# A two-layer transformer kernel: TensorE's order of work written out in layer 1's attention, and the projection's first step taken in parts

## The chip, the cores and the metric

The kernel runs on one core of one Trainium2 chip. The metric is the time of one execution on the device in microseconds (us). TensorE, VectorE, ScalarE and GpSimd (PE, DVE, ACT and POOL in the rows) compute, each from its own list of instructions; SyncE (SP) issues the transfers used here. They meet only at semaphores.

## The reference

Two layers over 1024 tokens of width 512. Each adds an attention and a feed-forward network, both computed from the same normalised input, to the residual:

```python
x = L0_attn_hidden_states
xn = _layernorm(x, axis=-1)
x = x + _L0_attn_ref(xn, ...) + _L0_ffn_ref(xn, ...)
xn = _layernorm(x, axis=-1)
x = x + _L1_attn_ref(xn, ...) + _L1_ffn_ref(xn, ...)
```

The change stands in layer 1, whose attention has 32 heads of 16 numbers; four heads share a key and a value:

```python
scores = jnp.einsum('bhqd,bhkd->bhqk', q, k)
scores = jnp.where(causal[None, None], -jnp.inf, scores)
weights = jax.nn.softmax(scores * (1.0 / HD ** 0.5), axis=-1)
ctx = jnp.einsum('bhqk,bhkd->bhqd', weights, v)
return jnp.dot(ctx, Wo) + bo
```

## The kernel before

Products that need the accuracy of float32 are made of three products of halves: every operand is split into a high part (ScalarE casts it) and a low part (GpSimd or VectorE subtracts), and `mm3` (lines 155 to 157) issues high by high, low by high and high by low.

**From layer 0's output to layer 1's queries** (`outputs_to_queries`). 32 steps, 16 for each half of the tokens, multiply the attention's output with a folded weight. A step has four slots to choose from (`s = k % 4`). ScalarE casts the outputs `ch` (line 2063) and then the weight `oh_w` (line 2064); the second cast raises `split_done`. VectorE then forms `cl` (line 2137) and GpSimd `ol_w` (line 2021). TensorE waits for both and issues twelve matmuls, three for each of four blocks of 128 tokens. Nothing can be multiplied before the first step's parts stand.

**Layer 1's attention** (`grouped_attention`). Eight rounds, one for each group `g` of four heads. A round does two things at once:

- For a group ahead it finds the largest score of every query. `score(g, v)` (line 2412) is a matmul for unit `v`, one of 4 heads by 8 tiles of 128 queries; a tile sees 128 to 1024 keys. VectorE reduces it (`maximum`, line 2505). Tiles come in the order of widths 640, 512, 768, 384, 896, 256, 1024, 128, over and over. The four wide ones (640, 768, 896, 1024) share one PSUM slot, the narrow ones another, so a score waits until the maximum of the score but one before it has been taken (`max_done`). A score wider than 512 is two matmuls.
- For its own group it computes the weights and the result in 12 steps `s`. `keys(g, s, p)` (line 2435) computes scores again, turned, for two heads; ScalarE takes the exponential (line 2526) from the same two banks, and `keys` of the next step waits for it. GpSimd clears the masked corner in 8 of 12 steps (line 2566). `weigh(g, s)` (line 2451) multiplies with the values, two steps later (`LAG`), and adds the sums of the weights in spare columns. The steps are 512, 384, 256, 128 queries wide, then five of 512 and 384, 256, 128.

TensorE's order is made by a rule: in step `s` stand `SHARE[s]` scores, about a third after `keys(g, s, 0)`, a third after `keys(g, s, 1)`, and the rest after `weigh`. With `SHARE = [4, 3, 2, 1, 4, 3, 4, 3, 4, 2, 1, 1]` a round holds 32 scores, and scores run 4 units ahead of the round.

At step 9 `turn` (line 2421) transposes the 32 columns of maxima into bank 0, `take_shift` on ScalarE copies them (line 2533), and SyncE carries them by four transfers into the queries' extra row (`shift_group`, line 1870). The next round's first `keys` waits for these. SyncE's loop for each round is: spread the sums of the group before (second half), then of this group (first half), then the shift, then the inverted sums (`spread_scales`), then the loads of the group three ahead. VectorE inverts a group's sums with `invert_sums` (line 2274) after its 25th maximum (`v == 24`). After the last step of rounds 3, 5 and 7 GpSimd scales two finished groups (`scale_heads`, line 2281). The last round has no scores; it begins the feed-forward network instead, one `mm3` for each step.

## Time and profile before

| | us |
|---|---|
| median of 3 runs | 1690.13 |
| lowest and highest run | 1683.23, 1690.16 |
| the profiled execution, its own time | 1686.73 |
| its span, first to last instruction | 1685.0 |

| stretch of the span (us) | what runs |
|---|---|
| 1068 to 1156 | the 32 steps of the projection |
| 1217 to 1488 | the eight rounds of layer 1's attention |
| 1489 to 1685 | layer 1's feed-forward network |

Of the whole span TensorE is busy 96%, VectorE 64%, ScalarE 51% and GpSimd 42%. The granted TensorE clock is 0.985 of full speed on average. "Busy" counts an engine's running instructions; TensorE's matmuls overlap, and their ends are modelled, so the starts of consecutive matmuls tell more than their lengths.

### The profile page before, as it was taken

To read this page: it belongs to the slowest core of one execution; us is meant where nothing else is said; L and a number is where in the kernel's file an instruction comes from. 1 tells how busy PE (TensorE), PEld (TensorE's weight loads), DVE (VectorE), ACT (ScalarE), POOL (GpSimd) and SP (SyncE) were. 2 spreads that over 40 slices of the span, in tenths; PEclk is the share of its full clock that TensorE was granted. 3 is DMA by queue.
4 is the path that set the end of the run, shared out by engine and by line. 5 is a ranking of instruction groups with operands and counts; after the bars stand their busy time and mean duration, and the time that the engine had idled before them with its cause. 6 is when DMAs were issued, how large, how long until landed. Compare 5 with 4: busy or idle time off the path is not lost. (4 is left out here: it accounts for less than half of the span.)

```text
span 1685.0 us, 27527 instructions
## 1 busy us (share of the span) xinstructions
PE 1610.0 (96%) x8810; PEld 1221.0 (72%) x8810; DVE 1083.1 (64%) x2489; ACT 851.7 (51%) x1592; POOL 714.2 (42%) x741
## 2 busy tenths in 40 slices
PE   6899999999998999999999999899899999999998
PEld 5688887788776777777777777687655555568887
DVE  3656657999937878887788877355767767310222
ACT  3456556444325655666566656443155655643321
POOL 1212213444656665666676665575011122232321
PEclk9999999999998999999999999999989999999999
DMA  8522323221110000001000100672523323131111
GB/s 247 187 80 82 94 70 102 65 62 37 57 32 7 27 25 20 20 26 32 20 20 26 33 13 14 195 223 68 156 56 62 72 59 69 49 102 51 51 50 50
DMA packets 113023, 114.17 MB, mean 68 GB/s; under 512 B 39777, under 2 KB 72001, under 8 KB 112897
## 3 DMA queue, kind: packets, MB, share of 16 engines
q1 hardware_dynamic: 110592, 108.40, 23.0%
q10 hardware_dynamic: 2304, 4.20, 0.7%
q8 instruction: 67, 1.10, 0.3%
q14 instruction: 60, 0.48, 0.1%
HBM read 83.97 MB, written 28.44 MB: 67 GB/s over the span
## 5 line engine op out<-in xcount | busy, mean ns | idle before, releaser
L1579 ACT ACTIVATE a_p<-a_sm,a_nmax 128x640 f32<-128x640 f32 (+7 forms) x256 | 198.5, 776 | 109.5 <-PE ps L1398 58.7
L1656 POOL TENSOR_SCALAR a_p<-a_p,a_rinv 128x640 f32<-128x640 f32 (+7 forms) x256 | 189.8, 750 | 125.8 <-DVE a_rinv L1490 125.7
L1479 DVE CUSTOM_DVE_ANT_0 a_sm<-ps,maskb 128x640 f32<-128x640 f32 (+7 forms) x256 | 189.6, 750 | 41.7 <-PE ps L1383 39.8
L2505 DVE CUSTOM_DVE_ANT_0 ga_sm<-ps,strip 128x640 f32<-128x640 f32 (+1 forms) x224 | 163.1, 754 | 72.0 <-PE ps L2412 70.5
L2526 ACT ACTIVATE ga_pt<-ps 128x1024 f32<-128x1024 f32 (+1 forms) x192 | 147.9, 810 | 113.2 <-PE ps L2435 112.2
L1398 PE MATMUL ps<-ident,a_p 128*128 128x128 f32 x1152 | 163.0, 276 | 2.7 <-DVE a_pt L1502 1.8
L2566 POOL TENSOR_SCALAR_AFFINE_SELECT ga_pt<-ga_pt 128x512 f32<-128x512 f32 x64 | 40.6, 635 | 265.7 <-ACT ga_pt L2526 265.5
L1398 PEld LDWEIGHTS ps<-ident,a_p 128*128 128x128 f32 x1152 | 133.2, 141 | 19.3 <-issue 6.6
L952 DVE SCALAR_TENSOR_TENSOR idx<-ix_r,ix_sgc,idx 128x256 f32<-128x256 f32 (+6 forms) x105 | 90.7, 884 | 74.2 <-ACT ix_r L918 74.2
L1418 PE MATMUL ps<-a_pt,vst 128*64 128x512 f32 (+3 forms) x768 | 134.2, 492 | 1.9 <-DVE a_pt L1502 1.1
L918 ACT ACTIVATE ix_r<-ps,ix_awc 128x256 f32<-128x256 f32 (+6 forms) x112 | 89.2, 798 | 83.1 <-PE ps L851 69.8
L1502 DVE COPY a_pt<-ps 128x128 f32<-128x128 f32 (+3 forms) x256 | 120.5, 482 | 14.5 <-PE ps L1398 14.2
L1383 PE MATMUL ps<-kh,lq_qh 128*128 128x512 f32 (+4 forms) x384 | 123.2, 375 | 6.7 <-POOL lq_ql L1793 3.6
L2412 PE MATMUL ps<-ga_kst,ga_qst 96*128 96x320 f32 (+1 forms) x336 | 107.5, 387 | 18.2 <-DVE ga_nmax L2505 15.6
L2412 PEld LDWEIGHTS ps<-ga_kst,ga_qst 96*128 96x128 f32 x336 | 58.0, 196 | 89.2 <-DVE ga_nmax L2505 64.0
L1383 PE MATMUL ps<-kh,lq_ql 128*128 128x512 f32 (+4 forms) x384 | 112.4, 347 | 0.0
L1383 PE MATMUL ps<-kl,lq_qh 128*128 128x512 f32 (+4 forms) x384 | 112.3, 347 | 0.0
L1594 ACT COPY a_pt<-ps 128x512 f32<-128x512 f32 x128 | 74.2, 580 | 64.8 <-PE ps L1398 63.6
L1418 PEld LDWEIGHTS ps<-a_pt,vst 128*64 128x64 f32 x768 | 51.5, 136 | 73.3 <-issue 64.9
L2435 PE MATMUL ps<-ga_qst,ga_kst 98*128 98x512 f32 (+3 forms) x384 | 99.2, 356 | 1.3 <-DMA ga_qst<-idx 1.3
L1780 POOL TENSOR_TENSOR lq_t<-lq_t 128x512 f32<-128x512 f32 x63 | 81.2, 1289 | 41.7 <-DVE lq_t L1775 41.7
L1793 POOL TENSOR_TENSOR lq_ql<-lq_t,lq_qh 128x512 fp32r<-128x512 f32 x64 | 82.3, 1286 | 28.1 <-ACT lq_qh L1787 28.0
(315 smaller groups left out, 3953.4 us busy)
## 6 DMA issues: line engine op xcount, KB each, us to landing
idx<-ctx_d SPq DMA_DIRECT2D x32, 256.0 KB, 3.2
idx<-wvo_d SPq DMA_DIRECT2D x32, 256.0 KB, 3.8
ga_qst<-qkd SPq DMA_DIRECT2D x42, 128.0 KB, 4.5
f_wr<-in_L_ffn_w SPq DMA_DIRECT2D x18, 256.0 KB, 2.7
x<-in_L_attn_hidden_states SPq DMA_DIRECT2D x16, 256.0 KB, 4.1
op_wo<-in_L_attn_o_w SPq DMA_DIRECT2D x8, 512.0 KB, 5.3
ix_w<-in_L_attn_idx_wq_w SPq DMA_DIRECT2D x64, 64.0 KB, 1.9
ix_fo<-in_L_attn_o_w SPq DMA_DIRECT2D x8, 512.0 KB, 4.1
```

The source lines that it names most:

```text
L952: ins = dve.scalar_tensor_tensor(out=acc, in0=r[:, u % 2, 0:W], scalar=sgc[:, a, t:t + 1], in1=acc, op0=ALU.mult, op1=ALU.add)
L1383: ins = pe.matmul(slots[kind][:, at0:at0 + k1 - k0], l[:, a, at], r[:, k0:k1], start=j == 0, stop=j == 2, skip_group_check=True)
L1398: ins = pe.transpose(ps[:, bank_t[n % NT], k * P:(k + 1) * P], p[kind][:, v // 2 % 2, (j0 + k) * P:(j0 + k + 1) * P], qwork["ident"][:, :])
L1418: ins = pe.matmul(ps[64 * a:64 * a + 64, bank_c, off:HALF], vst[:, j, :], pt[half][:, (2 * i + a) % NBUF, j, off:HALF], start=j == 0, stop ...
L1479: dve.tensor_tensor_reduce(out=in_row(sm[kind][:, 0:w], w), in0=in_banks(slots[kind], w), in1=in_row(maskb[:, MASK_OFF[t]:MASK_OFF[t + 1]] ...
L1502: dve.tensor_copy(pt[g][:, buf, j0:j0 + m, at], bank4(ps, bank_t[n % NT])[:, 0:m]).then_inc(pt_done[n % NT], 1)
L1579: act.activation(p[kind][:, v // 2 % 2, 0:w], sm[kind][:, 0:w], ACT.Exp, bias=nmax[:, v % 4:v % 4 + 1], scale=-1.0, accum_out=rsum[:, v % ...
L1656: pool.tensor_scalar(mine, mine, rinv[:, v % 4:v % 4 + 1], 1.0, ALU.mult, ALU.mult).then_inc(norm_done, 1)
L2412: ins = pe.matmul(slots[kind][:, at0:at0 + k1 - k0], qst[0:KQ, b, h // 2, t * P:(t + 1) * P], kst[0:KQ, b, h % 2, k0:k1], start=True, stop ...
L2435: ins = pe.matmul(ps[:, 2 * p + a, 0:q1 - q0], kst[0:KQ + 2, b, a, j * P:(j + 1) * P], qst[0:KQ + 2, b, p, q0:q1], start=True, stop=True)
L2505: dve.tensor_tensor_reduce(out=in_row(sm[kind][:, 0:w], w), in0=in_banks(slots[kind], w), in1=in_row(strip[:, S - w:], w), scale=-1.0, sca ...
L2526: act.activation(pt[:, n % RING, 2 * p:2 * p + 2, off:HALF], ps[:, 2 * p:2 * p + 2, 0:q1 - q0], ACT.Exp, scale=SCALE).then_inc(exp_done[p], 1)
```

## The change

Layer 0's attention already has its order written out before the change; the diff doesn't touch it. In layer 1:

1. The rule with `SHARE` goes. The 12 steps of a round are written out line by line: where each `keys`, score, `weigh` and `turn` stands.
2. Scores run further ahead. Four (`LEAD`) are issued ahead of round 0, and four more are added at the ends of the steps in `CATCH_UP`, three in round 0 and one in round 1, so that from round 2 on they run 8 units ahead.
3. `turn` stands ahead of `keys(g, 9, 1)`, `take_shift` between the two exponentials of step 9.
4. `weigh(g, 1)` stands one step earlier, in step 2, and step 3 has none.
5. `invert_sums` follows the 31st maximum (`v == 30`), and GpSimd's `scale_heads` stands ahead of step 4 of rounds 3, 5 and 7 rather than after step 11.
6. In the projection ScalarE casts the weight first and signals it by a semaphore of its own (`wvh_done`), for which GpSimd waits; the first step's twelve matmuls are issued by parts, four as soon as the high parts stand, four after `cl`, four after `ol_w`.

```diff
@@ outputs_to_queries @@
-                    pool.wait_ge(split_done[s], START + u + 1)
+                    pool.wait_ge(wvh_done[s], START + u + 1)
                     pool.tensor_tensor(ol_w[:, s], wr[:, s], f32(oh_w[:, s]), ALU.subtract).then_inc(wvl_done[s], 1)
...
-                    act.copy(ch[:, s], cr[:, s])
-                    act.copy(oh_w[:, s], wr[:, s]).then_inc(split_done[s], 1)
+                    act.copy(oh_w[:, s], wr[:, s]).then_inc(wvh_done[s], 1)
+                    act.copy(ch[:, s], cr[:, s]).then_inc(split_done[s], 1)
...
-                for half, k, s, u in steps:
+                def first_step():
+
+                    pe.wait_ge(wvh_done[0], START + 1)
+                    pe.wait_ge(split_done[0], START + 1)
+                    for t in range(4):
+                        pe.matmul(ps[:, t, :], ch[:, 0, t * P:(t + 1) * P], oh_w[:, 0], start=True, stop=False,
+                                  skip_group_check=True)
+                    pe.wait_ge(cl_done[0], START + 1)
...
+                    pe.wait_ge(wvl_done[0], START + 1)
...
+                first_step()
+                for half, k, s, u in steps[1:]:
@@ grouped_attention @@
-    LEAD = 3
+    LEAD = 4
+    TURN_AT = 9
...
-    SHARE = [4, 3, 2, 1, 4, 3, 4, 3, 4, 2, 1, 1]
+    CATCH_UP = ((0, 1), (0, 4), (0, 7), (1, 4))
...
-                        pe.wait_ge(exp_done[0], START + (g - 1) * NSTEP + NSTEP - LEAD + 1)
+                        pe.wait_ge(exp_done[0], START + (g - 1) * NSTEP + TURN_AT + 1)
...
+                for g in range(G1):
+                    keys(g, 0, 0)
+                    keys(g, 0, 1)
+                    next_score()
+                    next_score()
+                    next_weigh()
+                    end_step(g, 0)
...
-                        if v == 24 and g >= 2:
+                        if v == 30 and g >= 2:
                             invert_sums(dve, g - 2, rest)
...
                         exponential(g, s, 0)
+                        if s == TURN_AT and g + 1 < G1:
+                            take_shift(g + 1)
                         exponential(g, s, 1)
-                        if s == NSTEP - LEAD and g + 1 < G1:
-                            take_shift(g + 1)
...
+                        if s == 4 and g >= 3 and g % 2 == 1:
+                            scale_heads(pool, g // 2 - 1, ctxn, rest)
...
-                    if g >= 3 and g % 2 == 1:
-                        scale_heads(pool, g // 2 - 1, ctxn, rest)
```

The round as written out, in short: K is a `keys` of one pair of heads, W a `weigh`, T the `turn`, and a number is the width of a score, as they fall in rounds 2 to 5. Before, the same rounds read as in the second column.

| step | after | before |
|---|---|---|
| 0 | K K 640 512 W | K 896 K 256 W 1024 128 |
| 1 | K 768 K 384 W | K 640 K 512 W 768 |
| 2 | K 896 K 256 W 1024 W | K 384 K W 896 |
| 3 | K 128 K 640 512 | K K W 256 |
| 4 | K K 768 W 384 | K 1024 K 128 W 640 512 |
| 5 | K 896 K 256 W | K 768 K 384 W 896 |
| 6 | K 1024 128 K W 640 512 | K 256 K 1024 W 128 640 |
| 7 | K K 768 W 384 | K 512 K 768 W 384 |
| 8 | K 896 K W 256 1024 | K 896 K 256 W 1024 128 |
| 9 | K 128 W 640 T 512 K | K 640 K T W 512 |
| 10 | K 768 W 384 896 K | K K W 768 |
| 11 | K 256 W 1024 K 128 | K K W 384 |

TensorE at the start of round 3, from the first `keys` to the end of step 1. `ps<-ga_qst,ga_kst` is a `keys`, `ps<-ga_kst,ga_qst` a score, `ps<-ga_pt,v` a `weigh`. First as it stands before, then as it stands now:

```order
L2435 MATMUL ps<-ga_qst,ga_kst 128x512 x2
L2412 MATMUL ps<-ga_kst,ga_qst 128x512
L2412 MATMUL ps<-ga_kst,ga_qst 128x384
L2435 MATMUL ps<-ga_qst,ga_kst 128x512 x2
L2412 MATMUL ps<-ga_kst,ga_qst 128x256
L2451 MATMUL ps<-ga_pt,v 32x256 x4
L2412 MATMUL ps<-ga_kst,ga_qst 128x512 x2
L2412 MATMUL ps<-ga_kst,ga_qst 128x128
L2435 MATMUL ps<-ga_qst,ga_kst 128x384 x2
L2412 MATMUL ps<-ga_kst,ga_qst 128x320 x2
L2435 MATMUL ps<-ga_qst,ga_kst 128x384 x2
L2412 MATMUL ps<-ga_kst,ga_qst 128x512
```

```order
L2456 MATMUL ps<-ga_qst,ga_kst 128x512 x4
L2432 MATMUL ps<-ga_kst,ga_qst 128x320 x2
L2432 MATMUL ps<-ga_kst,ga_qst 128x512
L2472 MATMUL ps<-ga_pt,v 32x256 x4
L2456 MATMUL ps<-ga_qst,ga_kst 128x384 x2
L2432 MATMUL ps<-ga_kst,ga_qst 128x512
L2432 MATMUL ps<-ga_kst,ga_qst 128x256
L2456 MATMUL ps<-ga_qst,ga_kst 128x384 x2
L2432 MATMUL ps<-ga_kst,ga_qst 128x384
L2472 MATMUL ps<-ga_pt,v 32x128 x4
```

Before, only a 128-wide score and one `keys` stand between the 1024-wide score (512 x2) and the next wide one (320 x2); now the round starts with both `keys`, and its first wide score is followed by the 512-wide one, a `weigh` and a `keys` before the next wide one.

TensorE around the `turn` (`ps<-ident,ga_nmax`) in step 9 of round 3, before and now:

```order
L2412 MATMUL ps<-ga_kst,ga_qst 128x512 x2
L2412 MATMUL ps<-ga_kst,ga_qst 128x128
L2435 MATMUL ps<-ga_qst,ga_kst 128x384 x2
L2412 MATMUL ps<-ga_kst,ga_qst 128x320 x2
L2435 MATMUL ps<-ga_qst,ga_kst 128x384 x2
L2421 MATMUL ps<-ident,ga_nmax 32x128
L2451 MATMUL ps<-ga_pt,v 32x512 x4
```

```order
L2432 MATMUL ps<-ga_kst,ga_qst 128x512 x2
L2456 MATMUL ps<-ga_qst,ga_kst 128x384 x2
L2432 MATMUL ps<-ga_kst,ga_qst 128x128
L2472 MATMUL ps<-ga_pt,v 32x512 x4
L2432 MATMUL ps<-ga_kst,ga_qst 128x320 x2
L2442 MATMUL ps<-ident,ga_nmax 32x128
L2432 MATMUL ps<-ga_kst,ga_qst 128x512
L2456 MATMUL ps<-ga_qst,ga_kst 128x384 x2
```

The `weigh` has moved between the 1024-wide score and the next wide one, and the `turn` has moved ahead of step 9's second `keys`.

## Rows read from the trace of the kernel before

**Rows 1.** Stretches: length; PE, PEld, DVE, ACT, POOL busy (instructions); clock; DMA share; GB/s.

```profile
1222.00:1255.00 33.00, 30.70 (x152) 17.87 (x151) 21.75 (x59) 17.62 (x23) 3.80 (x6) 0.83 0.22 43
...
1288.00:1321.00 33.00, 30.41 (x197) 17.26 (x193) 23.75 (x65) 19.23 (x26) 5.03 (x8) 1.00 0.37 71
```

**Rows 2.** TensorE in order of time, one round: start, length, engine, line, operation, idle before.

```profile
1292.87 0.63 PE L2435 MATMUL ps<-ga_qst,ga_kst 98*128 98x512 f32 x2
1293.33 0.28 PE L2412 MATMUL ps<-ga_kst,ga_qst 96*128 96x256 f32 x1
1293.55 0.64 PE L2451 MATMUL ps<-ga_pt,v 128*32 128x256 f32 x8
1294.22 0.79 PE L2412 MATMUL ps<-ga_kst,ga_qst 96*128 96x512 f32 x3
1294.84 0.57 PE L2435 MATMUL ps<-ga_qst,ga_kst 98*128 98x384 f32 x2
1296.27 0.56 PE L2412 MATMUL ps<-ga_kst,ga_qst 96*128 96x320 f32 x2 [0.86 <-DVE ga_nmax L2505]
...
1304.41 0.79 PE L2412 MATMUL ps<-ga_kst,ga_qst 96*128 96x320 f32 x3 [0.23 <-DVE ga_nmax L2505]
...
1305.89 0.62 PE L2412 MATMUL ps<-ga_kst,ga_qst 96*128 96x512 f32 x2 [0.24 <-DVE ga_nmax L2505]
...
1307.57 0.68 PE L2412 MATMUL ps<-ga_kst,ga_qst 96*128 96x512 f32 x2
...
1309.44 0.73 PE L2412 MATMUL ps<-ga_kst,ga_qst 96*128 96x512 f32 x2
...
1320.43 1.07 PE L2451 MATMUL ps<-ga_pt,v 128*32 128x512 f32 x8
1321.42 0.50 PE L2412 MATMUL ps<-ga_kst,ga_qst 96*128 96x512 f32 x1
```

**Rows 3.** Who waited for whom in the eight rounds: total us, times, longest.

```profile
PE ps L2412 <- DVE ga_nmax L2505: 15.1, 30, 1.0
```

**Rows 4.** SyncE's transfers in order of time: start, time of issuing, line, destination, source.

```profile
1287.98 2.73 SPq L1870 DMA_DIRECT2D ga_qst<-idx  x4
...
1316.85 0.56 SPq L2248 DMA_DIRECT2D idx<-raw_d  x1
1321.40 2.75 SPq L1870 DMA_DIRECT2D ga_qst<-idx  x4
...
1421.69 2.76 SPq L1870 DMA_DIRECT2D ga_qst<-idx  x4
...
1453.97 2.75 SPq L1870 DMA_DIRECT2D ga_qst<-idx  x4
```

**Rows 5.** TensorE's last turn, and the first keys of the last round.

```profile
1453.35 0.28 PE L2421 MATMUL ps<-ident,ga_nmax 128*32 128x128 f32 x1 [0.73 <-DVE ga_nmax L2505]
...
1457.90 1.21 PE L2435 MATMUL ps<-ga_qst,ga_kst 98*128 98x512 f32 x4 [0.23 <-DMA ga_qst<-idx]
```

**Rows 6.** All engines in order of time, the projection's first step.

```profile
1067.78 0.62 ACT L2063 CAST oq_oh<-idx 128x512 fp32r<-128x512 f32 x1 [0.83 <-PEq L1367]
1068.30 0.61 ACT L2064 CAST oq_ol<-idx 128x512 fp32r<-128x512 f32 x1
...
1068.94 0.69 DVE L2137 TENSOR_TENSOR oq_oh<-idx,oq_oh 128x512 fp32r<-128x512 f32 x1 [11.87 <-ACT oq_ol L2064]
1068.99 3.46 POOL L2021 TENSOR_TENSOR oq_ol<-idx,oq_ol 128x512 fp32r<-128x512 f32 x2 [13.71 <-ACT oq_ol L2064]
...
1069.98 3.02 DVE L2137 TENSOR_TENSOR oq_oh<-idx,oq_oh 128x512 fp32r<-128x512 f32 x2 [0.34 <-ACT oq_ol L2064]
...
1070.91 0.77 PE L155 MATMUL ps<-oq_ol,oq_oh 128*128 128x512 f32 x1 [4.58 <-POOL oq_ol L2021]
```

**Rows 7.** All engines in order of time, the end of the last round.

```profile
1486.85 2.35 POOL L2281 TENSOR_TENSOR idx<-idx,sums 128x1024 f32<-128x1024 f32 x1
...
1488.79 0.34 SPq L2366 DMA_DIRECT2D raw_d<-raw  x1
```

More of the change, by code:

```diff
@@ L1964, in outputs_to_queries @@
          hi_done, lo_done, ones_done, formed) = (c.sem("oq_" + n) for n in names)
-        split_done, cl_done, wvl_done, used = (
-            c.sems(f"oq_{n}_", NS) for n in ("split_done", "cl_done", "wvl_done", "used"))
+        split_done, wvh_done, cl_done, wvl_done, used = (
+            c.sems(f"oq_{n}_", NS) for n in ("split_done", "wvh_done", "cl_done", "wvl_done", "used"))
         stored, w_in = c.sems("oq_stored", NT1), c.sems("oq_w_in", 2)
@@ L2219, in task @@
                             score(v)
-                for half, k, s, u in steps:
+                def first_step():
[5 more added lines that the diff above has]
+                    pe.wait_ge(cl_done[0], START + 1)
+                    for t in range(4):
+                        pe.matmul(ps[:, t, :], cl[:, 0, t * P:(t + 1) * P], oh_w[:, 0], start=False, stop=False,
+                                  skip_group_check=True)
+                    pe.wait_ge(wvl_done[0], START + 1)
+                    for t in range(4):
+                        ins = pe.matmul(ps[:, t, :], ch[:, 0, t * P:(t + 1) * P], ol_w[:, 0], start=False, stop=False,
+                                        skip_group_check=True)
+                    ins.then_inc(used[0], 1)
+                first_step()
+                for half, k, s, u in steps[1:]:
                     pe.wait_ge(cl_done[s], START + u + 1)
@@ L2431, in keys @@
                         pe.wait_ge(exp_done[p], START + g * NSTEP + s)
-                    if s == NSTEP - LEAD + 1 and g + 1 < G1 and p == 0:
+                    if s == TURN_AT + 1 and g + 1 < G1 and p == 0:
                         pe.wait_ge(nt_done, START + g + 2)
@@ L2454, in weigh @@
                     ins.then_inc(weighed, 1)
-                lead = sum(SHARE[NSTEP - LEAD:])
-                for v in range(lead):
-                    score(1, v)
-                for g in range(G1):
-                    done = lead
-                    for s in range(NSTEP):
-                        later = g + 1 if s < NSTEP - LEAD else g + 2
-                        first = done if s < NSTEP - LEAD else done - UNITS
-                        units = range(first, first + SHARE[s]) if later < G1 else range(0)
-                        done += SHARE[s]
-                        keys(g, s, 0)
-                        one, two = (len(units) + 1) // 3, (len(units) + 1) // 3 + len(units) // 3
-                        for v in units[:one]:
-                            score(later, v)
-                        keys(g, s, 1)
-                        for v in units[one:two]:
-                            score(later, v)
-                        if s == NSTEP - LEAD and g + 1 < G1:
-                            turn(g + 1)
-                        if g * NSTEP + s >= LAG:
-                            weigh((g * NSTEP + s - LAG) // NSTEP, (g * NSTEP + s - LAG) % NSTEP)
-                        for v in units[two:]:
-                            score(later, v)
-                        if g == G1 - 1:
-                            k, n = divmod(s, 2 * DT)
-                            if n == 0:
-                                pe.wait_ge(ahead["low"], START + k + 1)
-                            half, i = divmod(n, DT)
-                            at = slice(half * HALF, (half + 1) * HALF)
-                            ins = mm3(pe, ps[:, 4 + 2 * k + half, :], (ahead["h"][:, k, i], ahead["l"][:, k, i]),
-                                      (xnh[:, i, at], xnl[:, i, at]), i == 0, i == DT - 1)
-                            if i == DT - 1:
-                                ins.then_inc(ahead["hidden"], 1)
@@ L2489, in _, with next_score, next_weigh @@
-                for s in range(NSTEP - LAG, NSTEP):
-                    weigh(G1 - 1, s)
+                done, weighs = UNITS, -LAG
+                def next_score():
+                    nonlocal done
+                    if done < G1 * UNITS:
+                        score(done // UNITS, done % UNITS)
+                    done += 1
+                def next_weigh():
+                    nonlocal weighs
+                    if weighs >= 0:
+                        weigh(weighs // NSTEP, weighs % NSTEP)
+                    weighs += 1
@@ new lines, in end_step @@
+                def end_step(g, s):
+                    if (g, s) in CATCH_UP:
+                        next_score()
+                    if g == G1 - 1:
+                        k, n = divmod(s, 2 * DT)
+                        if n == 0:
+                            pe.wait_ge(ahead["low"], START + k + 1)
+                        half, i = divmod(n, DT)
+                        at = slice(half * HALF, (half + 1) * HALF)
+                        ins = mm3(pe, ps[:, 4 + 2 * k + half, :], (ahead["h"][:, k, i], ahead["l"][:, k, i]),
+                                  (xnh[:, i, at], xnl[:, i, at]), i == 0, i == DT - 1)
+                        if i == DT - 1:
+                            ins.then_inc(ahead["hidden"], 1)
@@ L2492, in _ @@
+                for n in range(weighs, G1 * NSTEP):
+                    weigh(n // NSTEP, n % NSTEP)
             @block.vector
```

84 lines of the change are left out of this document (82 added, 2 removed).

## The prediction

> **What bounds the kernel now.** I read the busy times by stretch first, then TensorE in order of time over one round, then the waits, then SyncE's transfers. In a middle round TensorE is busy 30.4 of 33 us at full clock, VectorE 23.8 and ScalarE 19.2 [rows 1]: TensorE is the bound, and the other two have slack on average. SyncE's shift transfers mark the rounds: three of them take 1421.69 - 1321.40 = 100.3 us, so a round is 33.43 us, and round 6 is 32.28 (1453.97 - 1421.69) [rows 4].
>
> What a round must take follows from starts of consecutive instructions [rows 2]. Two 512-wide `keys` take 1293.33 - 1292.87 = 0.46, 0.23 each. The 1024-wide and 128-wide scores together take 1294.84 - 1294.22 = 0.62, so a 128-wide one 0.15. A 256-wide `weigh` takes 0.67 (1293.55 to 1294.22), a 512-wide one 0.99 (1320.43 to 1321.42); by a straight line 0.83 at 384 and 0.51 at 128. A round has 18,432 columns of scores and as many of `keys`, 36 times 512 each: 8.3 + 8.3 us, plus 0.1 for each of the twelve 128-wide matmuls, 1.1. Of the twelve `weigh` six are 512 wide and two each 384, 256 and 128: 5.94 + 1.66 + 1.34 + 1.02 = 9.96. With the turn, 0.2, the work is 27.9. The other 5.5 us are waits and joints.
>
> Most are waits for VectorE before scores: 15.1 us of true idleness at the matmuls in 30 places [rows 3], more when the emptied pipeline is counted. They come from one rule. A wide score may not start until VectorE has taken the wide one before it. How long that is, start to start, the round shows where TensorE waited: 2.05 from 1024 to 640 (1294.22 to 1296.27), 1.48 from 640 to 768 (1304.41 to 1305.89), 1.87 from 896 to 1024 (1307.57 to 1309.44), and at most 1.68 from 768 to 896 (1305.89 to 1307.57) [rows 2]. In the old order too little work stands between: from step 0's 1024 to step 1's 640 only 0.46 + 0.15 + 0.35 = 0.96, short by 1.1, and the same from step 8 to 9. The other short places by the same sums: steps 0 and 1, 0.1 + 0.1; steps 4 to 5, 0.2 + 0.5; 5 to 6, 0.4; 6, 0.35. Together 3.85. Work and shortfalls make 31.75; the missing 1.7 of 33.43 I give to the joints around the twelve `weigh` (the 256-wide score ahead of one takes 0.22, 1293.33 to 1293.55, where its columns are worth 0.12), which stay.
>
> **Rounds 2 to 5, the written order.** The same sums in the new table: 640 to 768 in steps 0 and 1, 0.29 + 0.23 + 0.67 + 0.35 = 1.54, enough; 768 to 896, 1.6 and joints, enough; 896 to 1024 in step 2, 0.40 + 0.23 + 0.12 + 0.99 = 1.74 and a joint, about enough; 1024 to 640 in steps 2 to 3, 1.90 and a joint, about enough; in steps 6 and 8 to 9, 2.06 and 1.95, enough. Short remain 640 to 768 in steps 3 to 4 and 6 to 7 (1.44, 0.04 each), in 9 to 10 (1.20, short 0.28), and 1024 to 640 over the round's end (0.46 + 0.23 + 0.15 + 0.92 = 1.76, short 0.29). The `turn` now follows its 32nd maximum closely, with the reciprocal ahead of that maximum; I put 0.2. Sum 0.85. New round: 27.9 + 1.7 + 0.85 = 30.4, 3.0 less. Four rounds: -12.0. Bounds: all 5.5 us cannot go, since VectorE's own chain by the four start-to-start times is 7.1 for eight scores, 28.3 a round, and TensorE's work is 27.9; so at best 28.3 (-5.1 each, -20). From the other side the gain may be nothing.
>
> The place of `weigh(g, 1)` costs nothing: ahead of it stand a `keys`, a narrow score, a 0.99 `weigh` and a wide score after the exponential it needs, and GpSimd's masking, at 5.0 us in eight, 0.6 each [rows 1], fits. The moved `scale_heads` falls in the steps without masking; it was hidden before. The reciprocal at the 31st maximum comes some 2 us ahead of the shift, when the sums have long been issued.
>
> **SyncE.** Its loop from one shift to the last transfer of sums runs 1287.98 to 1317.41, 29.4 us, and then waits until 1321.40 [rows 4]. It has 4.0 us of slack, of which the shorter round takes 3.0. It stays hidden, by 1.0. Were it not, the round is bounded there at about 29.5 to 30.
>
> **Round 6** loses four scores more to the earlier rounds. It holds 24: 27.9 - 2.2 + 1.7 + 0.5 = 27.9. But from `turn` to the next round's `keys` 4.55 us pass at least (1453.35 to 1457.90, ended by the transfer) [rows 5], and behind the new `turn` stand only the `keys` of steps 9 to 11 and two `weigh`, 3.8: +0.7. So 28.6 for 32.3: -3.7 (bounds 0 and -4.4, without this wait).
>
> **Round 1** has one score more, and until step 4 its scores are one unit off the table: 1024 to 640 in step 3 has 0.23 + 0.15 + 0.46 = 0.84, short 1.2; 768 to 896 in step 5 short 0.6; two others 0.6. With the late places 3.0 short, for 3.85 before, and +0.25: -0.6. **Round 0** is four units off, and gets three more scores (+0.8). By the same sums steps 0 to 3 and 8 to 9 are short by 0.9, 1.1, 0.4, 1.0, 0.9 and 0.7, others by 1.7, 6.7 in all, of which the slow clock of its first part (0.83 granted over the stretch [rows 1]) hides perhaps 2: 4.7, for about 3.4 before. Round 0: +2.1 (bounds 0 and +4). **Round 7** has no scores; its work is the same: 0.
>
> **The projection's first step.** TensorE starts at 1070.91, when GpSimd's first product part stands (half of 3.46 after 1068.99) [rows 6]. Now the weight's cast is first, and both casts end at 1068.91 as before, so the first four matmuls start at about 1069.05: -1.9. After the long idle they run at the low level of the clock, 1.2 GHz (the first is 0.77 long, a single score at full speed 0.50 [rows 2, 6]), so at twice 0.23 four take 1.8, until 1070.85, and `cl`, 0.69 from 1068.94, stands by 1069.6. GpSimd starts 0.5 earlier and ends at 1070.2; the last four need it at 1072.7. The later steps' parts are made ahead of TensorE, so the 1.9 stays: -1.9 (bounds 0 and -2).
>
> The rows show VectorE and GpSimd in each other's way: beside GpSimd's subtractions VectorE's take 3.02 for two, 1.51 each, while the one that started first took 0.69 [rows 6]. The Trainium skill says the same (SBUF — State Buffer, in its passage on the port pair that VectorE and GpSimd share): whoever starts first holds the pair for its whole instruction and the other stands still. GpSimd now starts first, at 1068.4; by that rule `cl` comes at 1070.2 + 0.7 = 1070.9, 0.1 later than wanted, and the sum is 0.1 higher.
>
> **The end of round 7.** GpSimd's scaling ends at 1489.20, SyncE's last store at 1489.13 [rows 7]; taking the first away gives 0.1 at most: 0.
>
> Sum: -12.0 - 3.7 - 0.6 + 2.1 - 1.9 = -16.1, against the profiled execution's 1686.7: 1670.6. That execution is 3.4 below the median 1690.13, which two of three runs reach; I predict 1671.
>
> **Rivals.** (1) SyncE becomes the bound: in the new round its waits for landings lengthen, the shift comes late, and a round settles at 31.5 rather than 30.4. For: the slack is only 1.0. Against: most of the loop is issuing. Price: 4 x 1.1 and 1 in round 6: 1676.
>
> (2) The waits only change place. TensorE is recorded busy 30.4 of 33 us, so only 2.6 a round is idle, and if half of that is needed by the joints, four rounds give 5, round 6 gives 2, the first step 1.9 and round 0 takes 2: -7, 1680.
>
> (3) Slower: ScalarE's exponentials hold TensorE. In the new order `keys` of both pairs stand side by side in steps 0, 4 and 7, and across steps 9 to 10 and 10 to 11, and with them `keys` waits for the exponential that frees its banks, 19.23 us in some 26 instructions [rows 1], 0.74 each, plus about 0.3 of passing on. Five such places in eight rounds, 1.0 each, cost 40; less 16 gained, 1711. It decides from 0.4 for each place on. Against: at every one of them I count 0.8 to 2.5 us of TensorE's work since the keys whose exponential is needed.
>
> (4) Better: the places I call short are covered by the joints, and round 0 loses nothing: rounds of 29.5, 1665.
>
> **How the numbers follow.** Forecast 0.50, (1) 0.16, (2) 0.15, (3) 0.07, (4) 0.12. The forecast's own range is 1667 to 1675. The range 1662 to 1682 takes in (1), (2) and (4) and leaves (3) and tails, 0.15 to 0.2. What this measurement can tell from no change is 0.5%, 8.5 us, so below 1681.7 is faster: the forecast, (1), (4) and about half of (2), 0.84 with a little off for causes that I don't see, 0.82; same 0.11; slower 0.07.
>
> **What would show it.** Shift transfers 30.4 apart in rounds 2 to 5 for 33.4; no wait near 1 us before 320-wide scores there, and TensorE's waits for VectorE in the eight rounds down by more than half; round 0 longer by 2; the first projection matmul 2 us nearer to the first cast. SyncE waiting for the shift's maxima about 1 us a round shows (1) wrong; shift transfers waiting for nothing, and `keys` ended by the transfer of each round, show it right. Idle time before `keys` ended by ScalarE shows (3). A round above 32 would make the forecast wrong.

## The result, and the profile after

The changed kernel takes 1670.63 us (median of 4 runs, 1666.49 to 1672.89), the kernel before 1688.64 on the same chip (4 runs, 1683.23 to 1690.16): ratio 0.9896, 95% interval 0.9878 to 0.9914. The forecast was 1671. The profiled execution of the changed kernel took 1666.49, its span is 1664.8, its mean clock 0.988. A later set of runs gave 1666.89 for the changed kernel (6 runs) and 1686.80 for before (17 runs).

In the tables below a round runs from the first `keys` of one round to the first of the next.

| part (us) | before | changed | difference | forecast |
|---|---|---|---|---|
| first cast of the projection to the first `keys` | 152.93 | 149.11 | -3.8 | -1.9 |
| round 0 | 37.78 | 40.53 | +2.8 | +2.1 |
| round 1 | 33.43 | 32.29 | -1.1 | -0.6 |
| rounds 2 to 5, together | 133.70 | 120.39 | -13.3 | -12.0 |
| round 6 | 32.28 | 28.90 | -3.4 | -3.7 |
| round 7, to the restart of the feed-forward network | 31.69 | 31.84 | +0.15 | 0 |
| from there to the end | 195.41 | 195.41 | 0 | 0 |
| sum | | | -18.75 | -16.1 |

The other 1.4 us between the two spans lie ahead of the first cast, where nothing was changed. That part differs by more than this between executions: in the fourteen profiles of this document the first cast starts between 1064.2 and 1071.5, and ahead of it the granted clock was at its low level for 14 to 31 us in all. A difference of a few us between two spans or medians can come from there, so the comparisons below go by stretches.

Stretches of the changed kernel, columns as in [rows 1]:

```profile
1222.00:1255.00 33.00, 30.06 (x164) 15.66 (x164) 21.48 (x59) 15.55 (x22) 3.81 (x6) 0.90 0.09 19
1284.00:1314.00 30.00, 29.99 (x194) 17.04 (x193) 23.55 (x66) 19.25 (x28) 5.08 (x8) 1.00 0.38 73
```

In a middle round TensorE now has no idle time at all (29.99 of 30.00); in [rows 1] 2.6 of 33 us were idle. TensorE's waits over the same eight rounds as [rows 3]:

```profile
PE ps L2432 <- DVE ga_nmax L2605: 4.8, 9, 1.0
PE ps L156 <- PEq L2375: 1.5, 1, 1.5
PE ps L2442 <- DVE ga_nmax L2605: 0.7, 2, 0.4
PE ps L2456 <- DMA ga_qst<-idx: 0.6, 1, 0.6
PE ps L2432 <- ACT ga_pt L2626: 0.5, 1, 0.5
```

The waits for VectorE fell from 15.1 to 4.8 us, and those left are in rounds 0 and 1. The 1.5 us stand at the end of round 7, as before. One wait of 0.5 for ScalarE is what came of rival (3), which named 40 us. TensorE over the end of a round, as [rows 2]; first the turn, then the start of the next round:

```profile
1281.12 1.06 PE L2472 MATMUL ps<-ga_pt,v 128*32 128x512 f32 x8
1282.20 0.53 PE L2432 MATMUL ps<-ga_kst,ga_qst 96*128 96x320 f32 x2
1282.57 0.27 PE L2442 MATMUL ps<-ident,ga_nmax 128*32 128x128 f32 x1
...
1288.26 1.31 PE L2456 MATMUL ps<-ga_qst,ga_kst 98*128 98x512 f32 x4
1289.46 0.79 PE L2432 MATMUL ps<-ga_kst,ga_qst 96*128 96x320 f32 x3
1290.18 0.64 PE L2472 MATMUL ps<-ga_pt,v 128*32 128x256 f32 x8
```

In [rows 2] the 320-wide matmul of step 1 waited 0.86 for VectorE; here it has no idle time before it, nor has the `turn`. SyncE, as [rows 4]:

```profile
1313.37 2.74 SPq L1871 DMA_DIRECT2D ga_qst<-idx  x4
...
1342.23 0.57 SPq L2267 DMA_DIRECT2D idx<-raw_d  x1
1343.36 2.75 SPq L1871 DMA_DIRECT2D ga_qst<-idx  x4
...
1372.81 0.56 SPq L2267 DMA_DIRECT2D idx<-raw_d  x1
1373.46 2.07 SPq L1871 DMA_DIRECT2D ga_qst<-idx  x3
```

The shift transfers are 30.0 and 30.1 apart. The last transfer ahead of a shift ends 0.56 and 0.09 before it (1342.80 to 1343.36, 1373.37 to 1373.46), for 4.0 us before. The last turn and the first `keys` behind it, as [rows 5]:

```profile
1433.03 0.28 PE L2442 MATMUL ps<-ident,ga_nmax 128*32 128x128 f32 x1 [0.34 <-DVE ga_nmax L2605]
...
1437.55 1.19 PE L2456 MATMUL ps<-ga_qst,ga_kst 98*128 98x512 f32 x4 [0.57 <-DMA ga_qst<-idx]
```

4.52 us, as before (4.55); TensorE now runs out of work and waits 0.57 of them. The projection's first step, as [rows 6]; the four engines' rows are put one under another:

```profile
1066.33 0.62 ACT L2064 CAST oq_ol<-idx 128x512 fp32r<-128x512 f32 x1 [0.82 <-PEq L1368]
...
1067.03 4.66 POOL L2022 TENSOR_TENSOR oq_ol<-idx,oq_ol 128x512 fp32r<-128x512 f32 x3 [13.18 <-ACT oq_ol L2064]
1067.50 3.05 DVE L2138 TENSOR_TENSOR oq_oh<-idx,oq_oh 128x512 fp32r<-128x512 f32 x2 [11.86 <-ACT oq_oh L2065]
...
1067.61 1.79 PE L2227 MATMUL ps<-oq_ol,oq_oh 128*128 128x512 f32 x4 [2.72 <-ACT oq_oh L2065]
1069.20 1.91 PE L2231 MATMUL ps<-oq_ol,oq_oh 128*128 128x512 f32 x4
1070.91 1.28 PE L2235 MATMUL ps<-oq_ol,oq_oh 128*128 128x512 f32 x4
1072.02 0.39 PE L156 MATMUL ps<-oq_ol,oq_oh 128*128 128x512 f32 x1
```

The first matmul stands 1.28 us behind the first cast (1070.91 - 1067.78 = 3.13 in [rows 6]), and step 1 starts 5.69 behind it (8.39 before).

### The profile page after: what moved, and what is told of

Same layout as the page of the kernel before. It is cut to its first block and busy times, and to the rows that moved or that the text cites. A ratio compares the mean times of both kernels' runs of the same rounds, so it can differ in the third digit from the quotient of the medians.

```text
span 1664.8 us, 27535 instructions
## 1 busy us (share of the span) xinstructions
PE 1603.1 (96%) x8810; PEld 1217.1 (73%) x8810; DVE 1096.5 (66%) x2489; ACT 850.5 (51%) x1592; POOL 705.3 (42%) x741
## 5 line engine op out<-in xcount | busy, mean ns | idle before, releaser
L2432 PE MATMUL ps<-ga_kst,ga_qst 96*128 96x320 f32 (+1 forms) x336 | 101.6, 380 | 6.6 <-DVE ga_nmax L2605 5.3
```

Of the source, the lines that this page charges most:

```text
L2432: ins = pe.matmul(slots[kind][:, at0:at0 + k1 - k0], qst[0:KQ, b, h // 2, t * P:(t + 1) * P], kst[0:KQ, b, h % 2, k0:k1], start=True, stop ...
```

## The experiments

Each is compared with the kernel before on the same chip; runs 1 to 4, 5 to 8 and 9 to 12 shared the runs of before (1686.80, 1686.14 and 1686.92). "Rounds" are the lengths of rounds 0 to 7 in its profile. For the changed kernel they are 40.39, 32.35, 30.06, 30.10, 30.09, 30.10, 28.84, 31.83.

### 1 to 3: the changed kernel again, and its two halves

> The changed kernel once more, timed beside the others. The first four runs gave 1670.6 against 1688.6, -18.0, where the sum of the prediction was -16.1. If the profiled execution (1664.8 us of span) is the rule, the difference is -20; if the median is, -18. By the trace of the changed kernel rounds 2 to 5 take 30.10 us each from keys to keys (33.43 before), round 0 40.5 (37.8), round 1 32.3 (33.4), round 6 28.9 (32.3): that is -16.1 for the rounds and the rest from the projection. The rounds should repeat to 0.2 us each.

> The changed kernel with the projection as before: ScalarE casts the outputs first, GpSimd waits for both casts, and the first step is not taken in parts. Theory (the two parts add, each worth what the prediction gave it): 2 us slower than the changed kernel, 16 faster than before. Rival (the projection's stretch, 3.8 us shorter in the profiled execution, is all the edit's, because the clock rises to its full level earlier): 3.5 to 4 slower than the changed kernel.

> The kernel before with the projection's edit alone: weight cast first, first step in parts. Theory: 1.9 to 2 us faster than before, from the start of the first matmul, whose distance from the first cast goes from 3.1 to 1.3 us. Rival (clock): 3.5 to 4 faster. If neither, and the time is the same, a later step gives the gain back, since the loads of the fifth and later steps end at the same time.

```diff
--- attention only: the changed kernel, but
-                    act.copy(oh_w[:, s], wr[:, s]).then_inc(wvh_done[s], 1)
-                    act.copy(ch[:, s], cr[:, s]).then_inc(split_done[s], 1)
+                    act.copy(ch[:, s], cr[:, s])
+                    act.copy(oh_w[:, s], wr[:, s]).then_inc(split_done[s], 1)
...
-                first_step()
-                for half, k, s, u in steps[1:]:
+                for half, k, s, u in steps:
--- projection only: the kernel before, with these lines the other way round
```

| | median us (runs) | ratio, 95% interval |
|---|---|---|
| changed again | 1666.89 (6) | 0.9887, 0.9865 to 0.9910 |
| attention only | 1671.06 (6) | 0.9902, 0.9880 to 0.9924 |
| projection only | 1684.35 (12) | 0.9981, 0.9965 to 0.9996 |

With the attention alone the rounds are the changed kernel's (40.35, 32.34, 30.04, 30.11, 30.08, 30.11, 28.86, 31.84), and the stretch from the first cast to the first `keys` is before's, 153.01. With the projection alone that stretch is 149.14 and rounds 2 to 7 are before's, but for round 2 (34.84). Round 1 took 39.43 in that profile: from 1252 to 1270 its granted clock was 0.72 on average; in round 2 `keys` waited 1.5 for the shift's transfer, and from 1290 to 1295 the clock was 0.73. One row of TensorE ahead of the first of these two falls, and the stretch, columns as in [rows 1]:

```profile
1257.00 0.56 PE L2430 MATMUL ps<-ga_kst,ga_qst 96*128 96x320 f32 x2 [0.87 <-DVE ga_nmax L2523]
```

```profile
1252.00:1270.00 18.00, 16.64 (x82) 9.83 (x82) 9.32 (x26) 8.15 (x11) 2.86 (x5) 0.72 0.48 89
```

So the projection is worth 3.8 or 3.9 us in the profiles, by the stretch from the first cast to the first `keys`. The medians, in which the clock's falls are too, show 2.5 (the projection alone against before) and 4.2 (the attention alone against the changed kernel).

### 4: eight scores ahead from the start

> The changed kernel with all eight scores of lead issued ahead of round 0 and none added at the ends of steps, so that rounds 0 and 1 fall under the same table as the others. Theory (what is short in rounds 0 and 1 is that their scores stand off the table): round 0 loses the 3 scores and some 3 us of waits, round 1 one score and 2 us of waits; ahead of round 0 VectorE needs 2.9 us more for four maxima, of which 0.8 lie under the wait for the shift that is there now: 4 to 5 us faster than the changed kernel. Rival (the slow clock of the stage's start sets round 0, not the table): the four scores ahead cost 2 and nothing comes back: 0 to 2 us slower.

```diff
-    LEAD = 4
+    LEAD = 8
-    CATCH_UP = ((0, 1), (0, 4), (0, 7), (1, 4))
+    CATCH_UP = ()
```

1662.08 us (5 runs, 1659.23 to 1665.05), ratio 0.9849, 0.9825 to 0.9873: 4.8 less than the changed kernel in the same set, and the fastest version tried. The first `keys` comes 3.5 us later (152.56 after the first cast), and rounds 0 and 1 take 32.97 and 30.10 for 40.39 and 32.35; rounds 2 to 7 together are the same to 0.1 us (round 5 is 30.45 and round 6 28.64). The table of the order is only right for a lead of eight. Catching up inside rounds 0 and 1 makes them 7.4 + 2.2 us longer, by the four scores and by the waits, and the four scores in front cost 3.5. In the profile that is 6.1 us net, in the medians 4.8. Part of the 7.4 is the clock: it is low for some 17 us around the start of the attention in both profiles, but with eight ahead 7 us of that stand before the first `keys` rather than 4.

### 5: the new shares, placed by the old rule

> The kernel before with the changed kernel's number of scores in each step and eight scores ahead of round 0, but with the old rule that places them within a step (a third after the first keys, a third after the second, the rest after weigh), the turn, the weigh and the projection as before; the reciprocal at the 31st maximum. Theory (what counts is the work between one wide score and the next, not the number of scores in a step): the bookkeeping of the prediction finds 3.1 us short, mostly 1024 to 640 in steps 2 to 3 (0.95), 6 (640 to 768, 0.5), 8 to 9 (0.7) and 896 to 1024 in 10 to 11 (0.9), where the old order has 3.85 and the written one 0.85: rounds of 32.5 us in rounds 2 to 5. Rival (the shares did it): rounds within 0.5 of 30.1.

```diff
-    SHARE = [4, 3, 2, 1, 4, 3, 4, 3, 4, 2, 1, 1]
+    SHARE = [2, 2, 3, 3, 2, 2, 4, 2, 3, 3, 3, 3]
...
-                lead = sum(SHARE[NSTEP - LEAD:])
+                lead = 8
```

This is the kernel before with the new numbers of scores for each step, eight ahead, and the reciprocal at the 31st maximum. 1680.23 us (10 runs), ratio 0.9968, 0.9959 to 0.9978. Rounds 2 to 5 are 32.9, where the written order has 30.1 and the old shares 33.4. TensorE's waits:

```profile
PE ps L2412 <- DVE ga_nmax L2504: 16.8, 29, 1.0
```

This view starts at 1217 and so takes in two waits, 1.7 us, ahead of round 0; in the eight rounds themselves it is 15.1 us in 27 places, just what the kernel before has (15.1 in 30). So of 3.3 us for each round the shares and the lead give 0.5, and 2.8 come from the places within the steps: of the scores above all, with those of `turn` and of `weigh(g, 1)`, which run 5 leaves as before (for the latter see run 7).

### 6 and 12: the turn later, with four and with eight ahead

> The changed kernel with the turn behind keys(g, 9, 1) and the copy of the maxima behind both exponentials of step 9, as before. Theory (turn to next keys needs 4.55 us at least, and 5.6 us of work stand there now, 1.1 to spare; the late places take 0.6 and 0.8 of it): 0.3 to 0.5 a round, ended by the transfer at the first keys, and SyncE's loop, which now ends only 0.0 to 0.5 us ahead of the next maxima, shifts with it: rounds of 30.4 to 30.6, +2 to +3 us in all. Rival (the place doesn't matter, the order of scores does): rounds 30.1.

```diff
                     next_score()
-                    turn(g + 1)
                     next_score()
                     keys(g, 9, 1)
+                    turn(g + 1)
...
-                        if s == TURN_AT and g + 1 < G1:
-                            take_shift(g + 1)
                         exponential(g, s, 1)
+                        if s == TURN_AT and g + 1 < G1:
+                            take_shift(g + 1)
```

1680.00 us (10 runs), ratio 0.9963, 0.9952 to 0.9974: 13 over the changed kernel, where 2 to 3 were expected. Rounds 42.53, 38.87, 31.17, 31.13, 31.15, 31.18, 29.50, 31.84: 1.05 more in each of rounds 2 to 5, and 8.7 more in rounds 0 and 1. Most of those 8.7 are the clock, which was low for 3.4 us in round 0, behind a wait of 1.02, and for 13.7 us in round 1; at half the rate these cost up to 8.5 us, by estimate. First one row of TensorE in this kernel, then stretches of it, columns as in [rows 1]:

```profile
1265.95 0.56 PE L2432 MATMUL ps<-ga_kst,ga_qst 96*128 96x320 f32 x2 [1.04 <-DVE ga_nmax L2605]
```

```profile
1255.00:1265.00 10.00, 9.57 (x66) 5.75 (x65) 7.01 (x21) 5.85 (x10) 2.54 (x4) 1.00 0.73 132
1265.00:1267.00 2.00, 1.05 (x5) 0.95 (x6) 1.56 (x5) 0.22 (x1) 0.63 (x1) 0.94 0.20 70
1267.00:1279.00 12.00, 12.00 (x46) 6.03 (x44) 5.46 (x16) 6.51 (x7) 0.00 (x0) 0.50 0.11 35
```

Behind the wait of 1.04 us in round 1 the clock is at its low level, 1.2 GHz (0.50), for 13.7 us, with TensorE busy throughout. The changed kernel has the same wait at the same place of round 1, and in its profile the clock stayed:

```profile
1264.69 0.56 PE L2432 MATMUL ps<-ga_kst,ga_qst 96*128 96x320 f32 x2 [1.04 <-DVE ga_nmax L2605]
```

All ten executions with the late turn show a mean clock of 0.979 to 0.984; of the six of the changed kernel two do (0.984, 1670.3 and 1671.8 us), and four have 0.988 or 0.989 (1665.0 to 1667.6). Where the clock was low in executions that were not profiled isn't known: for the ten it may be round 1 as in the profile, and for the two it may as well be ahead of the first cast, as in the profile of run 2 (mean clock 0.983, nothing low in rounds 1 to 7, but 31 us low ahead of the cast). Run 12 asks whether the fall in round 1 hangs on round 1's wait. It has the edits of runs 4 and 6 together.

> The changed kernel with eight scores ahead of round 0, none added later, and the turn after both keys of step 9 (the two experiments with eight ahead and with the late turn, together). Theory (the late turn costs 1.0 us a round, because keys of the next round wait for the shift's transfer; the other 6 us that it cost were a fall of the clock to its low level after round 1's 1.04 us wait, a wait that eight ahead do away with): rounds 1 to 5 31.1 to 31.2 us, no clock below 1.00 in rounds 1 to 7, mean granted clock 0.987 or more, median 6 to 7 us over the version with eight ahead: 1668 to 1669. Rival (the fall comes from the idle time before keys, about 1 us in every round, and not from round 1's wait): a fall of the clock in one of the rounds, mean clock 0.983 to 0.985, 1674 to 1676.

1666.98 us (6 runs, clocks 0.987 to 0.990), ratio 0.9886, 0.9866 to 0.9906: no fall in the rounds of the profile, 4.9 over eight ahead alone. Rounds 33.83, 31.12, 31.09, 31.15, 31.11, 31.11, 29.46, 31.83. The sizes are as expected: in the profiles rounds 0 to 6 together are 6.5 longer than with eight ahead alone; the median is 1 us below the range. No clock below full speed shows from round 1 on, though each of rounds 0 to 6 has a wait of 1.01 or 1.02. The reason that this expectation gives for the 1.0 us in every round is wrong, as its rows show, first TensorE, then ScalarE:

```profile
1307.43 0.27 PE L2442 MATMUL ps<-ident,ga_nmax 128*32 128x128 f32 x1
1308.72 0.48 PE L2456 MATMUL ps<-ga_qst,ga_kst 98*128 98x256 f32 x2 [1.02 <-ACT idx L2633]
```

```profile
1307.63 0.81 ACT L2626 ACTIVATE ga_pt<-ps 128x768 f32<-128x768 f32 x1 [1.43 <-PE ps L2456]
1308.34 0.24 ACT L2633 COPY idx<-ps 32x128 f32<-32x128 f32 x1
```

It is not the next round's `keys` and not a transfer. The `turn` writes bank 0, so `keys` of step 10 must wait until ScalarE has copied the maxima away, and ScalarE has the second exponential first. In the changed kernel the turn, a 512-wide score and `keys(g, 9, 1)` stand in this order, and ScalarE copies ahead of that exponential: the copy is hidden behind the two. The kernel before also has its `turn` behind `keys(g, 9, 1)`, but a `weigh` and a score stand behind it there, and no wait for this copy shows in its rounds; so the 1.0 is what the late place costs in the new order, and not what moving the `turn` gained over the old one.

### 7: `weigh(g, 1)` back in step 3

> The changed kernel with weigh(g, 1) in step 3, behind its second keys, instead of in step 2. Theory (it only has to stand somewhere between the 1024-wide score and the next wide one, and it does in both): rounds 30.1, no difference beyond 0.5 us in all. Rival (its early place frees the buffer that the exponentials of step 4 wait for): 0.5 us a round, 3 to 4 in all.

```diff
                     next_score()
-                    next_weigh()
                     end_step(g, 2)
                     keys(g, 3, 0)
                     next_score()
                     keys(g, 3, 1)
+                    next_weigh()
```

1667.28 us (4 runs), ratio 0.9879, 0.9856 to 0.9903. Rounds 2 to 6 are 30.11, 30.06, 30.14, 30.09, 28.88: no difference, as the forecast's "costs nothing". Round 0 took 43.54 in this profile; the clock, low since the attention began, came back at about 1239 for 1227 in run 1. Round 1 is 31.37 for 32.35, shorter: there the scores stand off the table, a 1024-wide one just ahead of `keys(g, 3, 1)` and the next wide one, 640, behind it, and the `weigh` now stands between them. In run 1 the 640-wide one waits 1.04 us; here it has no idle time before it:

```profile
1267.31 0.85 PE L2472 MATMUL ps<-ga_pt,v 128*32 128x384 f32 x8
1268.09 1.00 PE L2432 MATMUL ps<-ga_kst,ga_qst 96*128 96x128 f32 x3
```

So with scores that catch up, the earlier `weigh` of change 4 costs 1.0 us in round 1, and it puts there the wait behind which run 6's clock fell.

### 8: the reciprocal back at the 25th maximum

> The changed kernel with the reciprocal of the sums after the 25th maximum, as before, rather than the 31st. With scores eight ahead the 25th maximum ends some 16.5 us after a round's first keys, and the sums of the second half land at about 19. Theory: VectorE stands for 2 to 2.5 us in each of rounds 2 to 6 and TensorE with it, since only one score can run ahead: rounds of 32, 8 to 12 us slower in all. Rival (VectorE's slack of 6 us a round takes it): no difference.

```diff
-                        if v == 30 and g >= 2:
+                        if v == 24 and g >= 2:
```

1667.34 us (4 runs), ratio 0.9886, 0.9865 to 0.9907: 0.5 over run 1 (of another set), where 8 to 12 were expected. Rounds 2 to 5 are 31.22, 30.53, 30.13, 30.11. The wait that the theory named is there, but it dies away. VectorE:

```profile
1306.63 0.35 DVE L2293 RECIPROCAL csum<-csum 128x32 f32<-128x32 f32 x1 [1.52 <-DMA csum<-raw_d]
...
1337.20 0.35 DVE L2293 RECIPROCAL csum<-csum 128x32 f32<-128x32 f32 x1 [0.85 <-DMA csum<-raw_d]
...
1367.33 0.35 DVE L2293 RECIPROCAL csum<-csum 128x32 f32<-128x32 f32 x1 [0.45 <-DMA csum<-raw_d]
...
1396.94 0.35 DVE L2293 RECIPROCAL csum<-csum 128x32 f32<-128x32 f32 x1
```

The theory put the wait at 2 to 2.5 us, where the first is 1.52, and multiplied it by the rounds. Why the sums come earlier from round to round was not tested; a stall of VectorE holds back the maxima and not SyncE's transfers of the sums, which would do it.

### 9: the cast order alone, without the parts

> The changed kernel with the projection's first step again as one block of twelve matmuls, as in the kernel before; ScalarE still casts the weight first and signals it by its own semaphore, and everything in the attention is as in the changed kernel. Theory (the parts and the order of the casts each gave something): the first matmul waits for both low parts, so it starts 2.6 to 2.9 us after the first cast (3.13 before, 1.28 changed); all twelve matmuls then run at the low clock, 5.3 us for 4.4, so step 1 starts 7.9 to 8.1 us after the first cast (8.39 before, 5.69 changed); the 1.1 us that the later steps gained through GpSimd's earlier signal stay. From the first cast to the first keys 151.2 to 151.6 us (152.93 before, 149.1 changed), median 2.2 to 2.5 us over the changed kernel. Rival 1 (order of the casts alone did it all): 149.1 to 149.6. Rival 2 (the parts alone did it, also the later gain): 152.5 to 153.

```diff
-                first_step()
-                for half, k, s, u in steps[1:]:
+                for half, k, s, u in steps:
```

1667.00 us (6 runs), ratio 0.9886, 0.9866 to 0.9905. The first matmul stands 2.57 us behind the first cast, step 1 7.85, the first `keys` 151.29: as the theory had it. The median is not 2.2 to 2.5 over the changed kernel's, as expected, but 0.1 over run 1's, from another set. Round 0 is 1.1 shorter here (39.32), since the clock came back 2.5 us nearer to its start, and the six mean clocks are 0.988 to 0.990, where two of run 1's six are 0.984. So of the 3.8 us the parts give 7.85 - 5.69 = 2.2, the order of the casts 8.39 - 7.85 = 0.5 in the first step and 144.54 - 143.44 = 1.1 in the 31 later ones, where GpSimd is signalled one cast earlier.

### 10: two more transfers for SyncE in each round

> The changed kernel with two more small transfers (4 KB each, of a weight to a spare buffer that nothing reads) issued by SyncE in each round ahead of its loads. Issuing one takes SyncE about 0.45 us, so its loop grows by 0.9 us. Theory (SyncE's loop is only 0.05 to 0.6 us shorter than the round of 30.1, and all of it is issuing or waiting for landings): the shift's transfer comes late, keys of the next round wait for it, and rounds 2 to 5 are 30.4 to 31.0 us instead of 30.1; rounds 1 to 6 cost 2 to 5 us in all. Rival (there is slack elsewhere in the loop, as the forecast's 1.0 us would have it): rounds stay at 30.1 and the median within 0.5 us of the changed kernel's.

```diff
+                    for k in range(2):
+                        sp.dma_start(spare[:, g, k], w1[0:P, 0:8]).then_inc(spare_in, 16)
```

1673.98 us (6 runs, 1666.97 to 1677.86), ratio 0.9912, 0.9886 to 0.9939. Neither theory: rounds 2 and 5 keep their 30.1, rounds 3 and 4 take 31.76 and 34.31. SyncE over round 3, then the first `keys` behind it, then the clock:

```profile
1318.95 2.74 SPq L1871 DMA_DIRECT2D ga_qst<-idx  x4
...
1346.48 3.04 SPq L2264 DMA_DIRECT2D csum<-raw_d  x4
...
1350.17 0.93 SPq L2405 DMA_DIRECT2D ga_spare<-in_L_ffn_inter_w  x2
1351.14 2.75 SPq L1871 DMA_DIRECT2D ga_qst<-idx  x4
```

```profile
1355.07 1.33 PE L2460 MATMUL ps<-ga_qst,ga_kst 98*128 98x512 f32 x4 [1.50 <-DMA ga_qst<-idx]
```

```profile
1357.00:1363.00 6.00, 6.00 (x30) 3.89 (x30) 2.94 (x8) 3.57 (x5) 1.27 (x2) 0.50 0.44 94
```

A round's loop with the two transfers is 30.2 us when its issues go as usual (the next one, 1351.14 to 1381.36), and `keys` bears a shift that is up to 1.2 late (from the turn to the next round's `keys` are 1288.26 - 1282.57 = 5.7 us, and the path needs 4.5). In round 3 some issues were slow (the sums took 3.04 for 1.7), the loop took 32.2, `keys` waited 1.50, and the clock fell behind that wait. Of the six executions two take 1667.0 and 1667.7 us at a clock of 0.99, the others 1672 to 1678 at 0.982 to 0.985. That the two are those in which this doesn't happen is likely and not shown: only one execution was profiled, and in it the first cast also came 6.4 us later than in run 1.

### 11: GpSimd's scaling back after step 11

> The changed kernel with GpSimd's scaling back after step 11 of rounds 3, 5 and 7. Theory (hidden in either place): rounds 2 to 6 unchanged to 0.1 us, and the time from the last keys of round 7 to the feed-forward network's restart unchanged to 0.3 us; the median within 0.5 us of the changed kernel's, apart from the spread of layer 0. Rival (the moved scaling is what keeps the end of round 7 free): the end is 0.5 to 1.5 us later.

```diff
-                        if s == 4 and g >= 3 and g % 2 == 1:
-                            scale_heads(pool, g // 2 - 1, ctxn, rest)
...
+                    if g >= 3 and g % 2 == 1:
+                        scale_heads(pool, g // 2 - 1, ctxn, rest)
```

1670.97 us (6 runs, clocks 0.983 and 0.986), ratio 0.9907, 0.9888 to 0.9927: 4 over run 9 of the same set, of which 2.1 stand in the parts below. Rounds 2 to 6 are unchanged, round 7 takes 32.45, 0.6 more, and the rest of the kernel 196.96, 1.5 more. The end of round 7 here, as [rows 7], and the clock behind it:

```profile
1468.75 2.34 POOL L2300 TENSOR_TENSOR idx<-idx,sums 128x1024 f32<-128x1024 f32 x1
...
1470.02 0.34 SPq L2386 DMA_DIRECT2D raw_d<-raw  x1
...
1471.44 0.47 PE L156 MATMUL ps<-xnh,ah_h 128*128 128x512 f32 x1 [2.09 <-PEq L2375]
```

```profile
1472.00:1474.00 2.00, 2.00 (x6) 1.61 (x5) 0.00 (x0) 1.97 (x3) 1.28 (x1) 0.50 0.71 198
```

The rival was right. In [rows 7] the scaling ended 0.07 behind the store; here it ends at 1471.09, 0.73 behind it, since in the written order the last `keys` of a round stands behind a `weigh`, and the last masking, ahead of the scaling, starts 29.2 us into round 7 for 28.4 before. TensorE idles 2.09 us for 1.46, and the clock falls to its low level for some 3 us.

## Why the prediction came out right, and where it was off

**The sum.** The parts moved by 18.75 us and the sum has 16.1: 1.9 are missing in the projection and 1.3 in rounds 2 to 5, and the other parts take some 0.6 back. That 1670.63 lies within 0.4 of the forecast of 1671 is partly luck. The sum was taken from one execution (1686.7); from the median of 1690.1 it would have given 1674. And three of the four executions of the changed kernel ran at a mean clock of 0.984 or 0.985; in the later set the median is 1666.9.

**Rounds 2 to 5** (forecast -12.0, measured -13.3). The mechanism is shown: 33.4 and waits of 15.1 us with the old order, 32.9 and again 15.1 us with the new shares under the old rule, 30.1 and no idle time in a middle round with the written order. The term that was too large is the 0.85 us of shortfalls left in the new round; the turn's 0.2 and the places short by 0.04 to 0.29 show no idle time. With work and joints at 29.6, half a microsecond of my sum remains that the rows don't separate.

**Round 6** (-3.7, -3.4). The path from the turn to the next `keys` was the end of it, 4.52 us with 0.57 of idle time at its end, for 0.7 forecast.

**Rounds 0 and 1** (+2.1 and -0.6; +2.8 and -1.1). The shortfalls had the right direction. Scores waited for VectorE 3.0 us in round 0 and 1.8 in round 1 (2.0 and 2.3 before), where 4.7 and 3.0 were counted (3.4 and 3.85). The length of round 0 also hangs on when the clock comes back: 39.3 in run 9, 40.5 here, 43.5 in run 7. That the waits need not be there at all, run 4 shows.

**The projection's first step** (-1.9, -3.8). This is the step that was mis-sized. Its own term was right, -1.85 for the first matmul. Two effects of the same edit were left out. The twelve matmuls took 5.26 us before and 4.41 changed, -0.85, since the clock comes back in their last third (the last three are 0.23 apart for 0.43 before) and the first is 0.31 ahead of the second for 0.57; started 1.3 us later, in one block, they took 5.28 (run 9). And "the later steps' parts are made ahead of TensorE" was wrong: 1.1 us were gained there by the earlier signal (run 9), and of TensorE's waits for GpSimd in the projection, 5.7 us in four places before (4.6 of them at the first matmul), none is left.

VectorE's first subtraction, 0.69 where it starts first [rows 6], takes about 1.4 when GpSimd has started 0.47 ahead of it. GpSimd, VectorE and TensorE in run 9:

```profile
1066.39 2.96 POOL L2022 TENSOR_TENSOR oq_ol<-idx,oq_ol 128x512 fp32r<-128x512 f32 x2 [13.18 <-ACT oq_ol L2064]
1066.86 3.04 DVE L2138 TENSOR_TENSOR oq_oh<-idx,oq_oh 128x512 fp32r<-128x512 f32 x2 [11.86 <-ACT oq_oh L2065]
1068.26 0.79 PE L156 MATMUL ps<-oq_ol,oq_oh 128*128 128x512 f32 x1 [4.01 <-DVE oq_oh L2138]
```

The first matmul is released by VectorE's first subtraction, which ends at 1068.2, 1.35 behind its start. The Trainium skill (SBUF — State Buffer, on the shared port pair) says that VectorE stands still until GpSimd's instruction is through. The trace agrees, roughly: GpSimd's first ends at 1067.66, and VectorE's 0.55 later, a little less than its 0.69. The forecast had GpSimd's instruction too long, 1.8 us for 1.27. In the changed kernel the second four matmuls waited for this subtraction by 0.2 us at their weights' load, and no delay is left at the matmuls, whose first starts 0.42 behind the one before, like the others.

**SyncE, rival (1).** The forecast gave it 1.0 us of slack and it did not become the bound. The measured slack of the loop is 0.1 to 0.6 us, and another 1.2 lies between turn and `keys`. Run 10 shows that this is near the edge: 0.9 us more of issuing, and a slow issue stops TensorE.

**Rival (2)** fell with the waits (29.99 of 30.00 busy), **rival (3)** with 0.5 us where 40 were named. **Rival (4)** had the rounds of 29.5 too short, but what it rests on, places called short that show no wait, is what rounds 2 to 5 have. That round 0 loses nothing was wrong.

**Edits costed at nothing.** `weigh` in step 2: nothing in rounds 2 to 6, but 1.0 us in round 1 (run 7). The reciprocal: 1.5 us in the profile by run 8, less than the spread. The scaling: beside the kernel before it is nothing (+0.15 over round 7), but with the new order it is worth 2.1 us (run 11, in the profiles). The forecast priced it against the old order alone, whose last masking came earlier.

## What to carry to other kernels

When one engine frees a buffer for another, measure start to start how long it takes, and put at least that much other work between two users of the buffer; how many pieces a step holds matters less than where they stand. Price an edit against the new order, not only the old: an engine hidden behind an end that has moved can come out as the end. A table of an order belongs to one lead, so start with that lead rather than catch up inside.

## What was not expected of the hardware

A short wait can stand ahead of a fall of the clock that costs far more than the wait. Behind waits of 0.87 and 1.47 us (run 3), 1.02 and 1.04 (run 6), 1.50 (run 10) and 2.09 (run 11) the granted clock fell to 1.2 GHz for about 10 and 3, 3 and 14, 10 and 3 us. Behind waits of 0.86 to 1.04 in most other rounds, and of 1.46 to 1.51 at the end of round 7 in the thirteen profiles other than run 11's, it did not. So the length of the wait alone doesn't decide it, and what does stays open; with rounds 0 and 1 free of VectorE's waits, the falls of run 6 were gone (run 12).

The spread of a kernel's executions goes with its mean clock: the changed kernel takes 1665.0 to 1667.6 at 0.988 and 0.989, and 1670.3 to 1671.8 at 0.984. But the places of the falls are not only where the change is. Of the low clock's time 14 to 31 us stand ahead of the projection, in code that is the same in every kernel here.
